# Turning x and s into columns on VectorE in 32x32 blocks, with their low parts found on GpSimd, in an attention and pooling kernel

## What is computed

```python
# layer 1: 16 heads of 16; seq1 = x, seq2 = side
query = seq2 + b_self
key   = concatenate([seq1 + b_prev, seq2 + b_self], 1)
value = concatenate([seq1, seq2], 1)
q, k, v = query @ Wq + bq, key @ Wk + bk, value @ Wv + bv       # split into heads
score_prev = einsum('bhqd,bhkd->bhqk', q, k[:, :, :l1]) * SCALE # masked by length
score_self = (q * k[:, :, l1:]).sum(-1, keepdims=True) * SCALE
weights = softmax(concatenate([score_prev, score_self], -1))
attn = weights[..., :-1] @ v[:, :, :l1] + weights[..., -1:] * v[:, :, l1:]
x = x + attn @ Wo + bo
# layer 2: pooling with one of three masks per batch
scores = tanh(x @ W1 + b1) @ v
p = softmax(where(mask, scores, -1e30))
x = x + (p @ x) / cnt
```

## Time and profile before

| | |
|---|---|
| time, median of 3 runs | 281.02 us (279.83 to 283.24) |
| the profiled execution | 281.62 us, of which the profile's span is 279.9 us |
| PE busy | 238.4 us, 85% of the span |
| DVE busy | 184.4 us, 66% |
| ACT busy | 156.6 us, 56% |
| POOL busy | 76.3 us, 27% |

### The profile page before, as it was taken

One profiled execution on the slowest core, in us unless ns is written; L12 is line 12 of the kernel. 1 busy time (PEld: TensorE's weight loads), 2 busy tenths in 40 slices (PEclk: granted clock), 3 DMA queues, 4 the chain that ended last, 5 costly groups with the idle time before them and its releaser, 6 DMA issues.

```text
span 279.9 us, 6089 instructions
## 1 busy us (share of the span) xinstructions
PE 238.4 (85%) x2100; PEld 187.4 (67%) x2100; DVE 184.4 (66%) x384; ACT 156.6 (56%) x297; POOL 76.3 (27%) x87
## 2 busy tenths in 40 slices
PE   2986898599979999999999989999999769886732
PEld 2984787367758777877788768777787455563622
DVE  2659655457469758875887588758985885335631
ACT  4351223376477557755785667557856546772430
POOL 8026011013025103610451035103511330316111
PEclk9999669599999999999999999999999997999977
DMA  5469636913865096609560946096409410011011
GB/s 152 103 235 233 138 112 182 210 31 115 242 142 188 5 248 134 228 16 252 119 227 20 256 108 225 18 246 118 150 33 261 95 72 2 8 34 37 0 40 37
DMA packets 28021, 35.50 MB, mean 127 GB/s; under 512 B 4440, under 2 KB 24416, under 8 KB 28000
## 3 DMA queue, kind: packets, MB, share of 16 engines
q1 hardware_dynamic: 27360, 33.12, 44.6%
q0 software_dynamic: 640, 2.10, 2.0%
HBM read 20.26 MB, written 14.69 MB: 125 GB/s over the span
## 4 chain that ended last, share of the span: by engine, by line
PE 59%; DVE 13%; DMA 9%; issue 8%; ACT 5%; SPq 3%; POOL 1%; ACTq 0%; DVEq 0%; POOLq 0%
PE ps_any L1080 20%; PE ps_any L1134 10%; PE ps_max L1108 9%; PE ps_any L1087 6%; DMA k_rows<-k_spill 5%; PE ps_exp L1121 4%; DVE s_max L887 4%; DMA k_spill<-k_lo 3%; PE ps_any L1184 3%; PE ps_any L1240 2%; DVE bv_cast L854 2%; SPq L418 1%; ACT pt L623 1%; PE ps_any L1200 1%; PE ps_any L1166 1%
## 5 line engine op out<-in xcount | busy, mean ns | idle before, releaser
L887 DVE TENSOR_REDUCE s_max<-ps_max 128x4 f32<-128x1024 f32 x64 | 78.1, 1220 | 25.1 <-PE ps_max L1108 25.1
L623 ACT ACTIVATE pt<-ps_exp 128x1024 f32<-128x1024 f32 x64 | 65.6, 1025 | 50.1 <-PE ps_exp L1121 49.5
L1108 PE MATMUL ps_max<-k_rows,q_rows 49*128 49x256 f32 x256 | 33.7, 343 | 13.0 <-DMA k_rows<-k_spill 7.2
L1108 PEld LDWEIGHTS ps_max<-k_rows,q_rows 49*128 49x128 f32 x256 | 20.2, 194 | 24.6 <-DVE s_max L887 10.4
L1134 PE MATMUL ps_any<-pt,v_aug 128*32 128x256 f32 x512 | 36.0, 401 | 0.0
L1121 PE MATMUL ps_exp<-q_rows,k_rows 51*128 51x256 f32 x256 | 27.0, 288 | 2.3 <-ACT pt L623 2.3
L578 POOL TENSOR_TENSOR attn<-num,rden 128x256 f32<-128x256 f32 x16 | 9.6, 621 | 54.0 <-DVE rden L1030 54.0
L1121 PEld LDWEIGHTS ps_exp<-q_rows,k_rows 51*128 51x128 f32 x256 | 20.3, 191 | 4.1 <-ACT pt L623 2.7
L569 POOL TENSOR_TENSOR prod_lo<-prod,prod_hi 128x512 fp32r<-128x512 f32 x8 | 10.3, 1282 | 42.2 <-ACT prod_hi L714 42.2
L1080 PE MATMUL ps_any<-st_hi,w_hi 128*128 128x256 f32 x64 | 20.9, 326 | 0.3 <-DVE st_lo L912 0.3
L1134 PEld LDWEIGHTS ps_any<-pt,v_aug 128*32 128x32 f32 x512 | 13.7, 112 | 10.5 <-issue 1.3
(11 more groups left out here) (145 smaller groups left out, 605.3 us busy)
## 6 DMA issues: line engine op xcount, KB each, us to landing
q_rows<-q_spill SPq DMA_DIRECT2D x32, 192.0 KB, 4.4
...
```

The costliest lines, as they stand in the source:

```text
L623: nc.scalar.activation(pt[:, 2 * j % 8:2 * j % 8 + 2], ps_exp[:], ACT.Exp).then_inc(p_ready, 1)
L887: nc.vector.tensor_reduce(s_max[:, j // MJ, :, :, j % MJ].rearrange("p t e -> p e t"), ps_max[:], AX.X, ALU.max).then_inc(max_found, 1)
L1108: last = pe.matmul(ps_max[:, e, t], q_rows[par][rows, j, P * t:P * t + P], k_rows[par][rows, j, :], start=True, stop=True)
```

## The change

From batch 1 on, x and s are no longer turned by TensorE. The DMA lays each batch out so that 32x32 blocks turned in place by VectorE give the columns, in the order "column 64a + 2c + k on partition 32a + c of half k". Four things go with it:

- loads: each of x and s comes in four DMAs of 32 partitions (runs of 64 numbers) where it was one of 128 partitions (runs of 256 numbers), s ahead of x. Wq, Wk and Wv are loaded in the matching order ("(p k) n"), Wq and Wk from ACT's queue;
- VectorE turns s in step 0 (`turn_s`) and x in step 1 (`turn_x`), two instructions of 128x256 each, into the new SBUF tensors `s_t` and `x_t`;
- `st_lo` and `xt_lo` move from VectorE to GpSimd, to steps 1 and 2, ahead of `vs_p`, which moves from step 1 to step 3;
- `TS` and `TX` go, `Q` moves from step 2 to step 3, `q_copy` and `q_lo` from step 3 to 4.

Batch 0 is still turned by TensorE, now into `ps_exp`, and its low parts are still made on VectorE.

```diff
-    "TS": (0, 1), "TX": (1, 1), "Q": (2, 1), "K": (5, 1), ...
+    "Q": (3, 1), "K": (5, 1), ...
-    ... "q_copy": (3, 1), ...
+    ... "q_copy": (4, 1), ...
-    "st_lo": (1, 1), "xt_lo": (3, 1), "prod": (8, 1), ...
+    "turn_s": (0, 1), "turn_x": (1, 1), "prod": (8, 1), ...
-    "vs_p": (1, -1), "q_lo": (3, 1), ...
+    "st_lo": (1, 1), "xt_lo": (2, 1), "vs_p": (3, -1), "q_lo": (4, 1), ...
...
+            def load_blocks(tile, dram, loaded, i, k):
+                blocks = row(dram, i, k)
+                for a in range(4):
+                    sp.dma_start(tile[32 * a:32 * a + 32, k % 2].rearrange("p n c k -> p n (c k)"), blocks[a]
+                                 ).then_inc(loaded[k % 2], 16)
...
-                    sp.dma_start(x_sb[:, par], row(x_rows, i, k)).then_inc(x_loaded[par], 16)
-                    sp.dma_start(s_sb[:, par], row(s_rows, i, k)).then_inc(s_loaded[par], 16)
+                    load_blocks(s_sb, s_blocks, s_loaded, i, k)
+                    load_blocks(x_sb, x_blocks, x_loaded, i, k)
...
+                    for c in at("st_lo", i, k, s) if not first else ():
+
+                        pool.wait_ge(st_hi_done, count(*c, 1, 1))
+                        nc.gpsimd.tensor_tensor(st_lo[:], s_t[:], st_hi[:].bitcast(F32), ALU.subtract
+                                                ).then_inc(st_lo_done, 1)
+                    for c in at("xt_lo", i, k, s) if not first else ():
+
+                        pool.wait_ge(xt_hi_done, count(*c, 1, 1))
+                        nc.gpsimd.tensor_tensor(xt_lo[:], x_t[:], xt_hi[:].bitcast(F32), ALU.subtract
+                                                ).then_inc(xt_lo_done, 1)
...
+            def turned(out_of, tile, par):
+
+                for kb in range(KB):
+                    last = nc.vector.transpose(out_of[:, kb].rearrange("p (n q) -> p n q", q=32), tile[:, par, :, :, kb])
+                return last
...
+                    for c in at("turn_s", i, k, s) if not first else ():
+
+                        dve.wait_ge(s_loaded[c[1] % 2], count(c[0] + c[1] // 2, 0, 32, 64 * (c[1] % 2)))
+                        if (n := count(*c, 1, 0)) is not None:
+                            dve.wait_ge(st_lo_done, n)
+                        turned(s_t, s_sb, c[1] % 2).then_inc(st_ready, 1)
...
-                    for c in at("TS", i, k, s):
-                        bank = take_bank("TS", *c)
-                        pe.wait_ge(s_loaded[c[1] % 2], count(c[0] + c[1] // 2, 0, 8, 16))
-                        transposed(bank, s_sb[:, c[1] % 2]).then_inc(st_ready, 1)
```

More of the change, by code:

```diff
@@ L55 @@
     "at_hi": (2, -2), "x1_hi": (5, -2), "x1t_hi": (6, -2), "tanh": (8, -2), "pool_p": (11, -2), "pt_hi": (13, -2),
-    "st_lo": (1, 1), "xt_lo": (3, 1), "prod": (8, 1), "group_max0": (8, 0), "group_max1": (16, 0),
+    "turn_s": (0, 1), "turn_x": (1, 1), "prod": (8, 1), "group_max0": (8, 0), "group_max1": (16, 0),
     "p_arg": (2, -1), "num": (14, -1),
@@ L60 @@
     "out": (16, -2),
-    "vs_p": (1, -1), "q_lo": (3, 1), "x1_lo": (5, -2), "prod_lo": (9, 1), "attn": (14, -1), "x_bo": (15, -1),
+    "st_lo": (1, 1), "xt_lo": (2, 1), "vs_p": (3, -1), "q_lo": (4, 1), "x1_lo": (5, -2), "prod_lo": (9, 1), "attn": (14, -1), "x_bo": (15, -1),
     "store": (16, -2),
@@ L102 @@
 BANK = {
-    "PV0": 2, "TS": 1, "MT1": 0, "AT": 3, "TX": 2, "Q": 0, "WO": 1, "PV1": 3, "X1T": 0, "K": 2, "KS": 1, "Z": 0,
+    "PV0": 2, "MT1": 0, "AT": 3, "Q": 0, "WO": 1, "PV1": 3, "X1T": 0, "K": 2, "KS": 1, "Z": 0,
     "PV2": 3, "MT0": 0, "SB": 2, "VS": 1, "SS": 0, "V": 2, "PV3": 3, "PT": 0, "NAT": 1, "NAT'": 0, "PO": 3,
@@ L649, in period @@
                             act.wait_ge(vs_ready, n)
-                        nc.scalar.activation(st_hi[:], ps_any[:, bank_of("TS", *c)], ACT.Copy
+                        nc.scalar.activation(st_hi[:], ps_exp[:, 0] if first else s_t[:], ACT.Copy
                                              ).then_inc(st_hi_done, 1)
@@ L775, in q_copy @@
                 last.then_inc(q_copied, 1)
+            for n in range(2):
+                load_weight(act, n)
             weight_hi(0)
@@ L908, in period @@
                 for s in range(STEPS + 1):
[L909 to L916 removed]
+                    for c in at("turn_s", i, k, s) if not first else ():
[3 more added lines that the diff above has]
+                        turned(s_t, s_sb, c[1] % 2).then_inc(st_ready, 1)
+                    for c in at("turn_x", i, k, s) if not first else ():
+                        dve.wait_ge(x_loaded[c[1] % 2], count(c[0] + c[1] // 2, 0, 32, 64 * (c[1] % 2)))
+                        if (n := count(*c, 1, 0)) is not None:
+                            dve.wait_ge(xt_lo_done, n)
+                        turned(x_t, x_sb, c[1] % 2).then_inc(xt_ready, 1)
+                    if first and s == 0:
+                        weight_lo(0)
+                        dve.wait_ge(st_hi_done, 1)
+                        nc.vector.tensor_tensor(st_lo[:], ps_exp[:, 0], st_hi[:].bitcast(F32), ALU.subtract
+                                                ).then_inc(st_lo_done, 1)
+                        split_bias_inputs()
+                        weight_lo(1)
+                        dve.wait_ge(xt_hi_done, 1)
+                        nc.vector.tensor_tensor(xt_lo[:], ps_exp[:, 1], xt_hi[:].bitcast(F32), ALU.subtract
+                                                ).then_inc(xt_lo_done, 1)
+                        setup_v()
+                        setup_biases()
+                        setup_masks()
+                        nc.vector.tensor_reduce(headsum[:], ident[:].rearrange("p (d j) -> p j d", j=NJ),
+                                                    AX.X, ALU.max).then_inc(headsum_ready, 1)
+                        weight_lo(2)
                     for c in at("at_lo", i, k, s):
@@ L1087, in transposed, with first_transposed @@
                         last = pe.transpose(out_of[:, kb, P * t:P * t + P], src[:, t, P * kb:P * kb + P], ident[:])
+                return last
+            def first_transposed(out_of, tile):
+                blocks = natural(tile).rearrange("p t (c k) -> p t k c", k=KB)
+                for kb in range(KB):
+                    for t in range(KB):
+                        last = pe.transpose(out_of[:, kb, P * t:P * t + P], blocks[:, t, kb], ident[:])
                 return last
```

73 lines of the change are left out of this document (29 added, 44 removed), and 2 rows, old and new, of the table REGULAR.

## The result

| | before | changed |
|---|---|---|
| time, median (lowest to highest) | 282.13 us (279.83 to 285.58) | 296.17 us (293.23 to 298.87) |
| ratio, 95% interval | | 1.049 (1.035 to 1.063) |
| the profiled execution, its span | 281.62, 279.9 us | 293.23, 291.6 us |
| mean granted clock of PE in it | 0.95 | 0.922 |

The forecast was 286.5 us with a range of 280.0 to 291.5; the time lies above it. Later, beside the last experiments, the same changed kernel gave 1.060 (1.055 to 1.066). The ratios leave out executions that ran slow, so they can differ a little from the quotient of the medians.

The account below looks back on a forecast made before the run. The prediction took GpSimd's queue, which delays `st_lo` and so `Q` and `max2`, to decide the change, with PE busy 85%. Terms 0.8 - 1.3 + 5.6 + 0.4 = +5.5 us gave 286.5 us, range 280.0 to 291.5.

Parts of the forecast that it names:

- B: Rival: GpSimd's queue is not in the way, `at_lo` decides when `max2` starts; 281.0 us, no change; chance 0.16.
- C: Rival: PE's relief from the removed transposes comes through, 8.8 us gained, 272.2 us; chance 0.07.
- D: Rival: VectorE's block transposes are slow, past 0.72 us each they delay `max2`; 298 us at 1.22 each; chance 0.08.
- the term of five periods: Batches 2 to 6: `st_lo` waits behind `x_bo` and the store on GpSimd, `Q` waits for it, `max2` later; +5.6 us.
- the load of `xr_sb` keeps its distance to the `max2` before it: Steady periods: the load moves with `max2`, so the delays of the five periods add up, to 5.56 us.
- From `max2` to the next period PE runs the same list: Steady periods: PE's list after `max2` is unchanged, so only the shift of `max2` counts there.
- Batch 1: Its period has no `x_bo` ahead, so `st_lo` is early and `Q` could start 1.6 us sooner; taken as -1.3 us.
- Batch 0 and the setup: `turn_s` stands ahead of batch 0's maxima, which PE waits for: +0.8 us; first-weight queues in the setup at 0.
- rival E: Loads in small runs ahead of the first spills on SP hold up the setup; 288.3 us; chance 0.07.
- Loads in steady periods at nothing: Eight DMAs for two cost SP 2.8 us more per batch, but `q_spill` behind them waits for later `Q` anyway: nothing.
- The `q_copy` wait: `X1T` takes the bank of `Q` and waits 0.08 us for `q_hi`, due in step 4; +0.4 us over five periods.
- the removed transposes lie beside the wait for `at_lo`: At PE's start of steady periods: `WO` needs `at_lo`, done at 110.90, so `max2` at 113.95 against 113.84; PE's gain taken away.

Follow-up runs that it names:

- the queue alone: Kernel before plus two spare GpSimd subtractions where the changed kernel has `st_lo` and `xt_lo`, `Q` behind `WO` and waiting for the first: 290.08 us, ratio 1.037.
- filled kernel: Changed kernel with eight transposes of the identity put back on PE where `TS` and `TX` stood: 292.98 us, ratio 1.051 to the kernel before.

## Why the prediction was wrong, step by step

**The mechanism was right, its size was not.** `st_lo` stands behind `x_bo` and the store, `Q` waits for it in batches 2, 3, 4 and 6, and the queue alone reproduces a loss of that size. B is out: `xr_sb` was waited for each time. C is out, D too: the block transposes took 0.42 us on average against 0.39 assumed and 0.72 needed for a tie. The step that failed is the term of five periods: +5.6 forecast, +10.1 measured up to `max2`. The parts, from the same rows in the five periods:

- `st_lo` ends later against `max0` than the sum had it: by -0.04, 0.30, 0.33, 0.21 and 0.53 us, together +1.3. The sentence "the load of `xr_sb` keeps its distance to the `max2` before it" fails: in batches 3, 4 and 6 `x_bo` started 24.96, 25.06 and 24.91 us behind that `max2`, where the rows had 24.25, 23.90 and 24.40. For batch 4's, SP issued the load 20.63 us behind that `max2`, where it had been 18.76.
- from the end of `st_lo` to `max2` it took 1.72, 2.96, 1.74, 2.45 and 2.03 us, where the sum has 1.53: +3.3. Some 0.15 each time is the step from `st_lo`'s end to the first matmul, the rest is mostly the clock; in batch 5 the last 0.2 us were VectorE's maxima, which ended at 178.73. The sum has no term for a lower clock: its 1.53 for `Q` is the pace at 2.4 GHz, and in batch 3 the 12 matmuls took 2.82 us at 1.2 GHz.

**"From `max2` to the next period PE runs the same list"** is true of the list and not of its duration: +2.1 us, nearly all in batches 3 and 6. In batch 6 it is the clock: PE was at 1.2 GHz until about 211.7, and the next maxima piece started 4.18 us behind `max2`, where it was 2.97. The fall came 1.2 us after a wait of 1.87 us, for `st_lo`, had ended (0.54 granted from 208.30 on). In batch 3 the clock makes only 0.25 of the 0.90 us; there the next `max0` waited 0.65 us for `k_rows`, which SP had issued 1.4 to 1.7 us later behind `max2` than before.

```profile
203.50:207.10 3.60, 1.67 (x12) 1.00 0.22 77
208.30:212.00 3.70, 3.70 (x30) 0.54 0.08 27
```

**Batch 1** was to gain 1.3 us. `Q` started 4.70 us behind `max0` (53.00 to 57.70) where it had been 6.35 (52.35 to 58.70), 1.65 us earlier and so as worked out (1.6). But PE was at 1.2 GHz from `max0` on (0.50 granted from 53.0 to 60.5), and the 12 matmuls of `Q` took 2.85 us in place of 1.61, so `max2` came 0.4 us earlier against `max0`.

```profile
57.70 0.58 PE L1118 MATMUL ps_any<-st_hi,w_hi 128*128 128x256 f32 x1
...
60.55 0.79 PE L1154 MATMUL ps_max<-k_rows,q_rows 49*128 49x256 f32 x4
```

**Batch 0 and the setup**: +0.8 was forecast for `turn_s` and nothing for the setup; +0.9 was measured up to the first `max0` and nothing for `turn_s`, which lay ahead of 3.5 us of DVE's idling (`max0` to `max2` of batch 0 took 5.70 us, before 5.88). That the two numbers are alike is luck. The +0.9 is rival E's mechanism: DVE's `k_lo` was ready at about 17.05, but SP had issued the eight loads until 17.8 and then the spills ahead of it, and spilled it at 20.74; before, it was spilled at 20.63, right when it was ready.

```profile
13.98 1.83 SPq L396 DMA_DIRECT2D s_sb<-in_fside_BxSxS  x4
...
15.85 1.93 SPq L396 DMA_DIRECT2D x_sb<-in_x  x4
16.18 0.87 DVE L1033 SCALAR_TENSOR_TENSOR k_lo<-ps_any,bqk_col,k_hi 128x256 fp32r<-128x256 f32 x2
...
20.74 0.73 SPq L419 DMA_DIRECT2D k_spill<-k_lo  x1
...
29.06 0.80 PE L1154 MATMUL ps_max<-k_rows,q_rows 49*128 49x256 f32 x4 [5.95 <-DMA k_rows<-k_spill]
```

The sign that was to mark E, a wait for a DMA past 30, was set too late: `max0` waited until 29.06 only because the new setup was sooner (`prod` on DVE at 15.38 and not 18.94) and so hid, as far as the two runs can be set side by side, most of the 3.0 us that the loads cost by themselves. That gain of the setup is not in the sum at all.

**Loads in steady periods at nothing** held. **The `q_copy` wait** was hardly there: `X1T` started 1.67 to 1.73 us behind `max2` in batches 2, 4 and 5, where it had been 1.67. **"PE's busy time falls by about 15"** failed, it fell by 5.0. The 15 doesn't follow from the prediction's own rows, which give 14 x 0.59 = 8.3; the rest of the difference fits the clock. "POOL's rises by 18" held. **That the removed transposes lie beside the wait for `at_lo`** failed: with six of eight gone and nothing added, 0.7 of their 0.9 us came through in each steady period. The change itself put `turn_s` and `turn_x` ahead of `at_lo`, and PE waited 0.63 to 0.83 us for `at_lo` in its steady periods.

**A term that is missing** is VectorE's waiting beside GpSimd, described at the end. In the changed kernel it decided only 0.2 us in batch 5, in the queue-alone kernel 0.7 us in each of two periods.

The parts don't form a sum. The queue alone costs 3.7% with the transposes still on PE, and taking six of eight away saves 0.9% by itself; the whole change costs 4.9 to 6.0%. Taken together, 2.1 to 3.2% is left for the rest. The filled kernel, at 1.051 beside 1.060, puts about 0.9 of it on the clock, with overlapping intervals; the setup is small in the profile (+0.9 us), and the remainder was not separated.
